# Transposes and grams of two chunks in one break of the TensorE stream, with two-step products on VectorE

## The chip, the cores and the metric

The kernel runs on one core of one Trainium2 chip. The metric is the device time of one execution in microseconds, from the core's first to its last instruction and what lies around it. Matmuls run on TensorE, elementwise work and reductions on VectorE, activations and copies out of PSUM on ScalarE. SyncE issues all DMAs. GpSimd only makes the identity matrix at the start.

## The reference

For each of 2048 rows there are 40 fields of 64 values. All 780 pairs of fields are multiplied elementwise, a small layer with ReLU gives each pair a score, a softmax over the pairs weighs the products, and the weighted sum goes through a last linear layer:

```python
p = x[:, ROW, :]            # ROW, COL: the 780 pairs i < j of 40 fields
q = x[:, COL, :]
inner = p * q
h = relu(einsum('bpe,he->bph', inner, W1) + b1)
logits = einsum('bph,oh->bpo', h, W2) + b2
attn = softmax(logits, axis=1)
pooled = sum(inner * attn, axis=1)
return pooled @ Wl.T + bl
```

All of it is float32.

## The kernel before

Two batch rows, one of each half of the batch, make a *duo*: its 2 x 64 embedding values fill the 128 partitions. A *step* is two duos, a *chunk* eight steps, a *round* 32 steps. There are 512 steps, 64 chunks and 16 rounds.

The work of a chunk: SyncE loads its rows (`load_chunk`, L193). TensorE transposes them with five 128x128 products (`turn_chunk`, L264) into a PSUM slot, and ScalarE copies them to `xt` (`copy_turned`, L353). VectorE appends the first 20 fields of each duo once more (`extend`, L409), so that each pair is a field and a field a fixed shift further, and makes a copy scaled by the last layer's weights (`scale_rows`, L418). TensorE multiplies that copy with `xt` into a 40x40 gram matrix per batch row (`gram_matrix`, L277, 32 products of 40 columns in a chunk). In the profile a float32 product is two records, in the listings of the order below it is one; a transpose is one in both. ScalarE copies the grams out (`copy_gram`, L361). SyncE stores them to DRAM in twelve DMAs (`store_gram`, L204), and loads a whole round of them again in the layout of the logits (`load_gram`, L216): with the gram in hand, the weighted sum and the last layer become a product of the softmax weights with gram entries.

The work of a step: VectorE makes the 2 x 780 pair products in `inner` (`products`: L431 twice, one for each half of the pairs, 760 elements per instruction; at each odd step L438 adds the last ten of each half for both steps). TensorE runs the first layer on them, half by half (`first_layer`, L296, 16 matmuls of 390 columns in a step), ScalarE adds the bias and applies ReLU (`relu`, L369, one per half), and TensorE adds the scores into the bank of the logits (`score`, L316, 8 matmuls), which holds a row for every step of the round. TensorE's order in step s is: layer of s, scoring of s-1, then, where the table names the step, the transposes of a chunk, then the grams of a chunk. ScalarE's order is the two relus, the copies of the same step, then an exponential where it is due.

At the end of a round VectorE copies the logits and takes maxima (`softmax_of_round`, L448 to L460, at step `KEEP_AT` = 7 of the next round), ScalarE takes the exponentials (L377, steps `EXP_AT`), and VectorE multiplies them with the gram and sums (`sums_of_round`, L468 and L476, steps `SUMS_AT`).

The order is written out by hand, by three tables from step to chunk (`turn_after`, `gram_after`, `spread_after`). The engines run freely against each other and are held by semaphores: `inner` is a ring of `INNER_RING` = 8 steps, `hidden` one of 4 steps, `xt` one of 3 chunks, `x_rows` and `gram_rows` have 2 places each, `x_scaled` one. Three PSUM slots are used in turn by everything that TensorE fills (each half of a layer, each chunk's transposes, each chunk's grams), so that each fill waits for the copy or relu of the fill three places before it:

```python
def wait_for_slot(*what):
    if place[what] >= SLOTS:
        pe.wait_ge(slots_emptied, place[what] - SLOTS + 1)
```

SyncE's queue for chunk n is: wait for the transposes of n, load chunk n+2, wait for the copied grams of n, store them; after the last chunk of a round, wait for all stores of the round and load the gram.

## Time and profile before

| | |
|---|---|
| median of 3 runs | 1144.26 us (1144.24 to 1145.02) |
| profiled execution | 1142.66 us |
| its span, first to last instruction | 1140.8 us |
| mean granted TensorE clock | 0.995 of full speed |
| busy: TensorE, VectorE, ScalarE | 1117.5, 1053.8, 981.2 us |
| instructions | 63299 |
| DMA traffic over the span | 45 GB/s |

Busy time counts the stretches in which at least one instruction of an engine is under way, and TensorE's products overlap: a layer record of 0.49 us has seven others beside it. So TensorE's pace is read from the starts of its groups in the timeline, not from the busy share or from the mean length of a record. A row of the timeline merges records of one kind that follow each other; its second number reaches to the modelled end of the last, which lies behind the start of the next group.

### The profile page before, as it was taken

The page shows a single profiled execution, that of the slowest core. Times are in us where ns is not written, and L with a number is a line of the kernel's source. Part 1 is how long each engine was busy: PE and PEld are TensorE (multiplying, and loading weights), DVE is VectorE, ACT ScalarE, POOL GpSimd, SP SyncE. Part 2 cuts the span into 40 slices and gives each one's busy share as a digit, 9 for nine tenths or more (in the row PEclk, how much of TensorE's full clock was granted, in tenths as well). Part 3 has the DMA queues.
Part 4 walks back from the last instruction along what each step waited for, and adds up shares of the span by engine and source line. Part 5 has one row for each costly group of instructions (what it writes and reads, how often), then busy time and mean ns, then how long its engine had stood idle before and what let it go on. Part 6 is the DMA issues. An engine that isn't in the chain of part 4 may idle for free.

```text
span 1140.8 us, 63299 instructions
## 1 busy us (share of the span) xinstructions
PE 1117.5 (98%) x29001; PEld 550.5 (48%) x29001; DVE 1053.8 (92%) x1691; ACT 981.2 (86%) x1219; POOL 0.7 (0%) x6
## 2 busy tenths in 40 slices
PE   6999999999999999999999999999999999999995
PEld 3445444444444444454544544554444444544442
DVE  7999999998999989999899998999999899998983
ACT  5888888888988888888888888888889888898884
POOL 0000000000000000000000000000000000000000
PEclk9999999999999999999999999999999999999998
DMA  2231211312212221122212113122131221222110
GB/s 58 39 70 26 67 30 35 67 29 63 41 29 63 41 56 35 29 65 39 58 35 68 29 34 70 28 64 41 25 67 36 58 39 29 63 41 57 23 25 23
DMA packets 220376, 51.31 MB, mean 45 GB/s; under 512 B 216016, under 2 KB 216016, under 8 KB 220112
## 3 DMA queue, kind: packets, MB, share of 16 engines
q1 hardware_dynamic: 220112, 47.27, 20.2%
q8 instruction: 229, 3.75, 1.4%
q14 instruction: 35, 0.29, 0.1%
HBM read 34.11 MB, written 13.12 MB: 41 GB/s over the span
## 4 chain that ended last, share of the span: by engine, by line
PE 98%; DVE 1%; SPq 1%; DMA 0%; ACT 0%; issue 0%; ACTq 0%
PE slot L296 60%; PE logit_bank L316 30%; PE slot L277 4%; PE slot L264 4%; DMA x_rows<-in_r_x 0%; PE slot L342 0%; SPq L193 0%; ACT hidden L369 0%; DVE weighted L468 0%; SPq L223 0%; SPq L227 0%; SPq L225 0%; SPq L230 0%; DVE logits L448 0%; DVE row_max L452 0%
## 5 line engine op out<-in xcount | busy, mean ns | idle before, releaser
L369 ACT ACTIVATE hidden<-slot,b_col 128x780 f32<-128x780 f32 x1024 | 874.7, 909 | 118.5 <-PE slot L296 118.5
L431 DVE TENSOR_TENSOR inner<-xt 128x760 f32<-128x760 f32 x1024 | 907.8, 943 | 51.3 <-PE slot L296 50.8
L296 PE MATMUL slot<-inner,w_block 64*32 64x390 f32 x16384 | 781.4, 489 | 0.0
L296 PEld LDWEIGHTS slot<-inner,w_block 64*32 64x32 f32 x16384 | 314.1, 107 | 331.0 <-issue 271.3
L316 PE MATMUL logit_bank<-hidden,w_window 64*32 64x390 f32 x8192 | 442.9, 487 | 0.6 <-ACT hidden L369 0.6
L316 PEld LDWEIGHTS logit_bank<-hidden,w_window 64*32 64x32 f32 x8192 | 155.3, 105 | 183.5 <-ACT hidden L369 85.6
L353 ACT COPY xt<-slot 128x640 f32<-128x640 f32 x64 | 44.3, 692 | 20.4 <-PE slot L264 20.4
L264 PE MATMUL slot<-ident,x_rows 128*128 128x128 f32 x320 | 50.1, 288 | 9.7 <-DMA x_rows<-in_r_x 9.7
L438 DVE TENSOR_TENSOR inner<-xt 128x80 f32<-128x80 f32 x256 | 59.4, 232 | 0.0
L264 PEld LDWEIGHTS slot<-ident,x_rows 128*128 128x128 f32 x320 | 34.6, 143 | 49.5 <-issue 44.1
L277 PE MATMUL slot<-xt,x_scaled 64*40 64x40 f32 x4096 | 52.9, 205 | 0.0
L277 PEld LDWEIGHTS slot<-xt,x_scaled 64*40 64x40 f32 x4096 | 45.4, 117 | 11.7 <-issue 11.7
L361 ACT COPY gram_rows<-slot 128x640 f32<-128x640 f32 x64 | 44.4, 693 | 5.9 <-PE slot L277 0.4
L418 DVE TENSOR_SCALAR x_scaled<-xt,wl_col 128x640 f32<-128x640 f32 x64 | 34.8, 544 | 0.0
L448 DVE COPY logits<-logit_bank 128x780 f32<-128x780 f32 x16 | 15.5, 970 | 20.5 <-PE logit_bank L316 20.5
L468 DVE CUSTOM_DVE_ANT_1 weighted<-weight,gram 128x380 f32<-128x380 f32 x32 | 28.0, 874 | 0.8 <-ACT weight L377 0.8
L409 DVE COPY xt<-xt 128x320 f32<-128x320 f32 x64 | 20.3, 317 | 5.8 <-ACT xt L353 5.8
L377 ACT ACTIVATE weight<-logits,exp_bias 128x390 f32<-128x390 f32 x32 | 19.9, 622 | 3.6 <-DVE exp_bias L460 3.6
L452 DVE TENSOR_REDUCE row_max<-logits 128x2 f32<-128x780 f32 x16 | 15.5, 966 | 0.5
L476 DVE CUSTOM_DVE_ANT_0 weighted<-weight,gram 64x10 f32<-64x10 f32 x64 | 10.8, 169 | 1.0
L342 PE MATMUL slot<-ident,stats 128*16 128x128 f32 x8 | 1.9, 416 | 6.0 <-DVE stats L483 6.0
L377 ACT ACTIVATION_READ_ACCUMULATOR weight<-logits,exp_bias 128x1 f32 x32 | 6.4, 201 | 0.0
(28 smaller groups left out, 27.0 us busy)
## 6 DMA issues: line engine op xcount, KB each, us to landing
x_rows<-in_r_x SPq DMA_DIRECT2D x128, 160.0 KB, 3.1
gram<-gram_dram SPq DMA_DIRECT2D x32, 400.0 KB, 3.8
gram_dram<-gram_rows SPq DMA_DIRECT2D x512, 12.5 KB
gram_dram<-gram_rows SPq DMA_DIRECT2D x256, 25.0 KB
w_rows<-in_L_rec_W SPq DMA_DIRECT2D x2, 16.0 KB, 2.3
wl_col<-in_L_rec_Wl SPq DMA_DIRECT2D x2, 0.2 KB, 2.3
b_col<-in_L_rec_b SPq DMA_DIRECT2D x2, 0.2 KB, 2.3
w_window<-in_L_rec_W SPq DMA_DIRECT2D x2, 0.2 KB, 2.3
```

What stands on the lines that cost most here:

```text
L264: last = nc.tensor.transpose(banks_of("turn", n)[:, t * P:(t + 1) * P], x_rows[n % 2][:, t, :, :].rearrange("p h e -> p (h e)"), ident[:, :])
L277: last = nc.tensor.matmul(banks_of("gram", n)[j * TILE:j * TILE + FIELDS, at:at + FIELDS], x_scaled[rows, duo * FIELDS:(duo + 1) * FIELDS] ...
L296: last = nc.tensor.matmul(banks[to:to + QUAD, ab * BANK:ab * BANK + HALF], w1_block[rows, of:of + QUAD], inner[rows, at:at + HALF], start= ...
L316: last = nc.tensor.matmul(logit_bank[g * QUAD:(g + 1) * QUAD, j * BANK:j * BANK + HALF], w2_window[rows, first:first + QUAD], hidden[s % R ...
L353: nc.scalar.copy(window_view(xt[n % XT_RING], 0, [[EXT, CHUNK_DUOS], [TT, U], [1, TT]]), window_view(banks_of("turn", n), 0, [[U, CHUNK_DU ...
L361: nc.scalar.copy(gram_rows[n % 2][:, :, :, :].rearrange("p a m n -> p a (m n)"), banks_of("gram", n)[:, :].rearrange("p (a n) -> p a n", a ...
L369: nc.scalar.activation(hidden[s % RING][:, half * PAIRS:(half + 1) * PAIRS].rearrange("p (a n) -> p a n", a=2), banks_of("layer", s, half) ...
L377: nc.scalar.activation(weight[:, j * HALF:(j + 1) * HALF], logits[:, j * HALF:(j + 1) * HALF], ACT.Exp, bias=exp_bias[:, j:j + 1], accum_o ...
L418: nc.vector.tensor_scalar(x_scaled[:, :].rearrange("p (d f) -> p d f", f=FIELDS), whole[:, :, 0:FIELDS], wl_col[:, 0:1], None, ALU.mult).t ...
L431: nc.vector.tensor_tensor(window_view(inner, to + half * HALF, [[PAIRS, STEP_DUOS], [SPAN, SHIFTS], [1, SPAN]]), window_view(fields, at + ...
L438: nc.vector.tensor_tensor(window_view(inner, to + SHIFTS * SPAN, [[PAIRS, duos], [HALF, 2], [1, LAST]]), window_view(fields, at, [[EXT, du ...
L468: nc.vector.tensor_tensor_reduce(out=weighted[:, 0:main].rearrange("p (d i) -> p d i", i=SPAN), in0=weight[:, of:of + main].rearrange("p ( ...
```

## The change

The chunks are taken in groups of two. The transposes and the grams of a group are issued together, once in sixteen steps: at step 16g - 12 the transposes of chunks 2g and 2g+1 (10 products), and behind them the grams of chunks 2g-2 and 2g-1 (64 products). ScalarE copies them in the same order, two and two. `xt` has four places, `x_scaled` two, `inner` sixteen steps. VectorE makes the products of two steps in one instruction per half, in the order first half, the last ten, second half, so that the layer's first half waits for two instructions and the second for three. The extension and scaling of a chunk are at step 15 of a group and at step 3 of the next, the exponentials at steps 3 and 7 of a round in place of 4 and 5, the sums at 15 and 21 in place of 13 and 14. SyncE loads both chunks of a group, then stores both.

```diff
--- before.py
+++ after.py
@@ -48,8 +48,9 @@
     U = FIELDS // TT
 
     RING = 4
-    INNER_RING = 8
-    XT_RING = 3
+    INNER_RING = 16
+    XT_RING = 4
+    GROUP = 2
     SLOTS = 3
 
     BANK = 512
@@ -82,7 +83,7 @@
         x_rows = [sb(f"x_rows{s}", [P, TT, 2, EMBED]) for s in range(2)]
         xt = [sb(f"xt{s}", [P, CHUNK_DUOS * EXT]) for s in range(XT_RING)]
         inner = sb("inner", [P, INNER_RING * STEP])
-        x_scaled = sb("x_scaled", [P, CHUNK_DUOS * FIELDS])
+        x_scaled = [sb(f"x_scaled{s}", [P, CHUNK_DUOS * FIELDS]) for s in range(GROUP)]
         gram_rows = [sb(f"gram_rows{s}", [P, 2, GRAM_PAIRS, FIELDS]) for s in range(2)]
         gram = sb("gram", [P, STEP_DUOS * SPAN * FIELDS])
         hidden = [sb(f"hidden{s}", [P, STEP]) for s in range(RING)]
@@ -145,18 +146,23 @@
         gram_dram = nc.dram_tensor("gram_dram", (ROUNDS, STEP_DUOS, 2, 2, ROUND_STEPS, SPAN, FIELDS), F32,
                                    kind="Internal").ap()
 
-        def inner_to(s):
-
-            return 5 * (s // 2 + 1)
-
-
-        TURN_AT = -13
-        GRAM_AT = -5
-        SPREAD_AT = -3
-
-        gram_after = {max(n * CHUNK_STEPS + GRAM_AT, 1 + n): n for n in range(CHUNKS)}
-        turn_after = {n * CHUNK_STEPS + TURN_AT: n for n in range(2, CHUNKS)}
-        spread_after = {max(n * CHUNK_STEPS + SPREAD_AT, 1 + n): n for n in range(1, CHUNKS)}
+        def inner_to(s, half):
+
+            return 3 * (s // 2) + 2 + half
+
+
+
+        GROUP_STEPS = GROUP * CHUNK_STEPS
+        TURN_AT = -12
+        GRAM_AT = TURN_AT + GROUP_STEPS
+        SPREAD_AT = [-1, 3]
+
+        def chunks_of(group):
+            return range(group * GROUP, (group + 1) * GROUP)
+
+        gram_after = {g * GROUP_STEPS + GRAM_AT: g for g in range(CHUNKS // GROUP)}
+        turn_after = {g * GROUP_STEPS + TURN_AT: g for g in range(1, CHUNKS // GROUP)}
+        spread_after = {n // GROUP * GROUP_STEPS + SPREAD_AT[n % GROUP]: n for n in range(1, CHUNKS)}
 
 
         place = {("turn", 0): 0, ("weights", 0): 1, ("turn", 1): 2}
@@ -164,9 +170,11 @@
             place["layer", s, 0] = len(place)
             place["layer", s, 1] = len(place)
             if s in turn_after:
-                place["turn", turn_after[s]] = len(place)
+                for n in chunks_of(turn_after[s]):
+                    place["turn", n] = len(place)
             if s in gram_after:
-                place["gram", gram_after[s]] = len(place)
+                for n in chunks_of(gram_after[s]):
+                    place["gram", n] = len(place)
 
         def count_to(*what):
 
@@ -177,8 +185,8 @@
 
 
         KEEP_AT = 7
-        EXP_AT = [4, 5]
-        SUMS_AT = [13, 14]
+        EXP_AT = [3, 7]
+        SUMS_AT = [15, 21]
 
         x_chunks = x.rearrange("(h c b) f e -> h c (b f e)", h=2, b=CHUNK_DUOS).rearrange(
             "h c (p t e) -> h c p t e", p=P, t=TT)
@@ -232,13 +240,15 @@
             for column, value in ((b2_col, b2), (bl_col, bl)):
                 sp.dma_start(column[:, :], value.rearrange("(h o) -> h o", o=1).to_broadcast([P, 1])).then_inc(
                     offsets_loaded, 16)
-            for n in range(CHUNKS):
-                if n + 2 < CHUNKS:
-                    sp.wait_ge(slots_filled, count_to("turn", n))
-                    load_chunk(n + 2)
-                store_gram(n)
-                if n % CHUNKS_PER_ROUND == CHUNKS_PER_ROUND - 1:
-                    load_gram(n // CHUNKS_PER_ROUND)
+            for group in range(CHUNKS // GROUP):
+                for n in chunks_of(group):
+                    if n + 2 < CHUNKS:
+                        sp.wait_ge(slots_filled, count_to("turn", n))
+                        load_chunk(n + 2)
+                for n in chunks_of(group):
+                    store_gram(n)
+                    if n % CHUNKS_PER_ROUND == CHUNKS_PER_ROUND - 1:
+                        load_gram(n // CHUNKS_PER_ROUND)
 
             sp.wait_ge(y_ready, 1)
             sp.dma_start(y_dram, y_out[:, :].rearrange("r (a k) -> r a k", a=2)).then_inc(y_stored, 16)
@@ -276,14 +286,13 @@
                             at = ab * BANK + m * FIELDS
                             last = nc.tensor.matmul(
                                 banks_of("gram", n)[j * TILE:j * TILE + FIELDS, at:at + FIELDS],
-                                x_scaled[rows, duo * FIELDS:(duo + 1) * FIELDS],
+                                x_scaled[n % GROUP][rows, duo * FIELDS:(duo + 1) * FIELDS],
                                 xt[n % XT_RING][rows, duo * EXT:duo * EXT + FIELDS], start=True, stop=True,
                                 tile_position=(ab * TILE, j * TILE))
                 last.then_inc(slots_filled, 1)
 
             def first_layer(s, half):
-                if half == 0:
-                    pe.wait_ge(inner_ready, inner_to(s))
+                pe.wait_ge(inner_ready, inner_to(s, half))
                 wait_for_slot("layer", s, half)
                 banks = banks_of("layer", s, half)
                 for j in range(STEP_DUOS):
@@ -331,9 +340,11 @@
                 if s:
                     score(s - 1)
                 if s in turn_after:
-                    turn_chunk(turn_after[s])
+                    for n in chunks_of(turn_after[s]):
+                        turn_chunk(n)
                 if s in gram_after:
-                    gram_matrix(gram_after[s])
+                    for n in chunks_of(gram_after[s]):
+                        gram_matrix(n)
             score(STEPS - 1)
 
             pe.wait_ge(stats_kept, ROUNDS)
@@ -348,7 +359,7 @@
                 act.wait_ge(slots_filled, count_to("turn", n))
                 if n >= XT_RING:
 
-                    act.wait_ge(inner_ready, inner_to((n - XT_RING + 1) * CHUNK_STEPS - 1))
+                    act.wait_ge(inner_ready, inner_to((n - XT_RING + 1) * CHUNK_STEPS - 1, 1))
                     act.wait_ge(slots_filled, count_to("gram", n - XT_RING))
                 nc.scalar.copy(window_view(xt[n % XT_RING], 0, [[EXT, CHUNK_DUOS], [TT, U], [1, TT]]),
                                window_view(banks_of("turn", n), 0, [[U, CHUNK_DUOS], [1, U], [P, TT]])).then_inc(
@@ -387,9 +398,11 @@
                 relu(s, 0)
                 relu(s, 1)
                 if s in turn_after:
-                    copy_turned(turn_after[s])
+                    for n in chunks_of(turn_after[s]):
+                        copy_turned(n)
                 if s in gram_after:
-                    copy_gram(gram_after[s])
+                    for n in chunks_of(gram_after[s]):
+                        copy_gram(n)
                 for j in range(STEP_DUOS):
                     r, after = (s - EXP_AT[j]) // ROUND_STEPS, (s - EXP_AT[j]) % ROUND_STEPS
                     if r > 0 and after == 0:
@@ -411,35 +424,35 @@
             def scale_rows(n):
                 if n == 0:
                     dve.wait_ge(wl_loaded, 2 * 16)
-                else:
-
-                    dve.wait_ge(slots_filled, count_to("gram", n - 1))
+                if n >= GROUP:
+
+                    dve.wait_ge(slots_filled, count_to("gram", n - GROUP))
                 whole = xt[n % XT_RING][:, :].rearrange("p (d f) -> p d f", f=EXT)
-                nc.vector.tensor_scalar(x_scaled[:, :].rearrange("p (d f) -> p d f", f=FIELDS), whole[:, :, 0:FIELDS],
+                nc.vector.tensor_scalar(x_scaled[n % GROUP][:, :].rearrange("p (d f) -> p d f", f=FIELDS), whole[:, :, 0:FIELDS],
                                         wl_col[:, 0:1], None, ALU.mult).then_inc(scaled_ready, 1)
 
             def products(s):
+
                 n, in_chunk = s // CHUNK_STEPS, s % CHUNK_STEPS
                 if in_chunk == 0:
                     dve.wait_ge(xt_ready, n + 1)
                 if s >= INNER_RING:
-                    dve.wait_ge(slots_filled, count_to("layer", s - INNER_RING, 1))
-                fields = xt[n % XT_RING]
+                    dve.wait_ge(slots_filled, count_to("layer", s + 1 - INNER_RING, 1))
+                fields, duos = xt[n % XT_RING], 2 * STEP_DUOS
                 to = (s % INNER_RING) * STEP
                 at = in_chunk * STEP_DUOS * EXT
                 for half in range(2):
                     nc.vector.tensor_tensor(
-                        window_view(inner, to + half * HALF, [[PAIRS, STEP_DUOS], [SPAN, SHIFTS], [1, SPAN]]),
-                        window_view(fields, at + half * SPAN, [[EXT, STEP_DUOS], [0, SHIFTS], [1, SPAN]]),
-                        window_view(fields, at + half * SPAN + 1, [[EXT, STEP_DUOS], [1, SHIFTS], [1, SPAN]]),
+                        window_view(inner, to + half * HALF, [[PAIRS, duos], [SPAN, SHIFTS], [1, SPAN]]),
+                        window_view(fields, at + half * SPAN, [[EXT, duos], [0, SHIFTS], [1, SPAN]]),
+                        window_view(fields, at + half * SPAN + 1, [[EXT, duos], [1, SHIFTS], [1, SPAN]]),
                         ALU.mult).then_inc(inner_ready, 1)
-                if s % 2:
-                    to, at, duos = to - STEP, at - STEP_DUOS * EXT, 2 * STEP_DUOS
-                    nc.vector.tensor_tensor(
-                        window_view(inner, to + SHIFTS * SPAN, [[PAIRS, duos], [HALF, 2], [1, LAST]]),
-                        window_view(fields, at, [[EXT, duos], [SPAN + LAST, 2], [1, LAST]]),
-                        window_view(fields, at + SPAN, [[EXT, duos], [SPAN + LAST, 2], [1, LAST]]),
-                        ALU.mult).then_inc(inner_ready, 1)
+                    if half == 0:
+                        nc.vector.tensor_tensor(
+                            window_view(inner, to + SHIFTS * SPAN, [[PAIRS, duos], [HALF, 2], [1, LAST]]),
+                            window_view(fields, at, [[EXT, duos], [SPAN + LAST, 2], [1, LAST]]),
+                            window_view(fields, at + SPAN, [[EXT, duos], [SPAN + LAST, 2], [1, LAST]]),
+                            ALU.mult).then_inc(inner_ready, 1)
 
             def softmax_of_round(r):
                 dve.wait_ge(steps_scored, (r + 1) * ROUND_STEPS)
@@ -489,7 +502,8 @@
             dve.memset(w2_window[:, :], 0.0).then_inc(zeroed, 1)
             extend(0)
             for s in range(STEPS):
-                products(s)
+                if s % 2 == 0:
+                    products(s)
                 if s == 1:
                     scale_rows(0)
                 if s in spread_after:
```

TensorE's order around the break at step 11 before. The rows are line, operation, output and input tile, shape and count; `slot` under L264 takes transposes, under L277 grams, under L296 the layer:

```order
L316 MATMUL logit_bank<-hidden,w_window 32x390 x8
L296 MATMUL slot<-inner,w_block 32x390 x16
L316 MATMUL logit_bank<-hidden,w_window 32x390 x8
L264 MATMUL slot<-ident,x_rows 128x128 x5
L277 MATMUL slot<-xt,x_scaled 40x40 x32
L296 MATMUL slot<-inner,w_block 32x390 x16
L316 MATMUL logit_bank<-hidden,w_window 32x390 x8
```

and now, around the break at step 20:

```order
L325 MATMUL logit_bank<-hidden,w_window 32x390 x8
L305 MATMUL slot<-inner,w_block 32x390 x16
L325 MATMUL logit_bank<-hidden,w_window 32x390 x8
L274 MATMUL slot<-ident,x_rows 128x128 x10
L287 MATMUL slot<-xt,x_scaled 40x40 x64
L305 MATMUL slot<-inner,w_block 32x390 x16
L325 MATMUL logit_bank<-hidden,w_window 32x390 x8
```

The transposes and grams stand together twice as long, half as often.

ScalarE's order around the break at step 35 (step 3 of round 1) before:

```order
L369 ACTIVATE hidden<-slot,b_col 128x780 x16
L353 COPY xt<-slot 128x16x40
L361 COPY gram_rows<-slot 128x640
L369 ACTIVATE hidden<-slot,b_col 128x780 x2
L377 ACTIVATE weight,round_stats<-logits,exp_bias 128x390
L369 ACTIVATE hidden<-slot,b_col 128x780 x2
L377 ACTIVATE weight,round_stats<-logits,exp_bias 128x390
L369 ACTIVATE hidden<-slot,b_col 128x780 x12
```

and now, from step 21 on, around the break at step 36 (step 4 of round 1):

```order
L380 ACTIVATE hidden<-slot,b_col 128x780 x30
L388 ACTIVATE weight,round_stats<-logits,exp_bias 128x390
L380 ACTIVATE hidden<-slot,b_col 128x780 x2
L364 COPY xt<-slot 128x16x40 x2
L372 COPY gram_rows<-slot 128x640 x2
L380 ACTIVATE hidden<-slot,b_col 128x780 x6
L388 ACTIVATE weight,round_stats<-logits,exp_bias 128x390
```

The copies stand two and two, and one exponential stands two relus ahead of them, where both stood behind.

VectorE's order around an extension, before:

```order
L431 TENSOR_TENSOR inner<-xt 128x2x380 x4
L438 TENSOR_TENSOR inner<-xt 128x8x10
L409 COPY xt<-xt 128x16x20
L418 TENSOR_SCALAR x_scaled<-xt,wl_col 128x640
L431 TENSOR_TENSOR inner<-xt 128x2x380 x4
L438 TENSOR_TENSOR inner<-xt 128x8x10
```

and now, around those at step 15 and 19:

```order
L445 TENSOR_TENSOR inner<-xt 128x4x380 x2
L451 TENSOR_TENSOR inner<-xt 128x8x10
L445 TENSOR_TENSOR inner<-xt 128x4x380
L422 COPY xt<-xt 128x16x20
L431 TENSOR_SCALAR x_scaled<-xt,wl_col 128x640
L445 TENSOR_TENSOR inner<-xt 128x4x380
L451 TENSOR_TENSOR inner<-xt 128x8x10
L445 TENSOR_TENSOR inner<-xt 128x4x380 x2
```

Products of two steps are two instructions of 4 duos and one for the last ten, where they were four of 2 duos and one.

## Rows read from the trace of the kernel before

**Rows 1.** The page: busy time by engine; granted TensorE clock in 40 slices, in tenths.
```profile
PE 1117.5 (98%) x29001; PEld 550.5 (48%) x29001; DVE 1053.8 (92%) x1691; ACT 981.2 (86%) x1219; POOL 0.7 (0%) x6
...
PEclk9999999999999999999999999999999999999998
```

**Rows 2.** The page: chain that ended last, by engine and line.
```profile
PE slot L296 60%; PE logit_bank L316 30%; PE slot L277 4%; PE slot L264 4%; DMA x_rows<-in_r_x 0%; PE slot L342 0%; SPq L193 0%; ACT hidden L369 0%; DVE weighted L468 0%; SPq L223 0%; SPq L227 0%; SPq L225 0%; SPq L230 0%; DVE logits L448 0%; DVE row_max L452 0%
```

**Rows 3.** Timeline of TensorE around one break: start us, us, engine, line, what, count.
```profile
525.20 0.87 PE L316 MATMUL logit_bank<-hidden,w_window 64*32 64x390 f32 x16
525.99 0.77 PE L264 MATMUL slot<-ident,x_rows 128*128 128x128 f32 x5
526.69 0.83 PE L277 MATMUL slot<-xt,x_scaled 64*40 64x40 f32 x64
527.45 1.54 PE L296 MATMUL slot<-inner,w_block 64*32 64x390 f32 x32
528.78 0.86 PE L316 MATMUL logit_bank<-hidden,w_window 64*32 64x390 f32 x16
529.44 1.52 PE L296 MATMUL slot<-inner,w_block 64*32 64x390 f32 x32
...
538.62 0.86 PE L316 MATMUL logit_bank<-hidden,w_window 64*32 64x390 f32 x16
```

**Rows 4.** Timeline of TensorE at the start: the first layer.
```profile
12.51 3.68 PE L296 MATMUL slot<-inner,w_block 64*32 64x390 f32 x64
```

**Rows 5.** Timeline of TensorE at the start of a round.
```profile
572.02 1.52 PE L296 MATMUL slot<-inner,w_block 64*32 64x390 f32 x32
573.45 0.89 PE L316 MATMUL logit_bank<-hidden,w_window 64*32 64x390 f32 x16
```

**Rows 6.** Timeline of TensorE, cut at 508.90 and 509.05 us: the transposes' ends.
```profile
508.59 0.55 PE L264 MATMUL slot<-ident,x_rows 128*128 128x128 f32 x3
...
508.59 0.66 PE L264 MATMUL slot<-ident,x_rows 128*128 128x128 f32 x4
```

**Rows 7.** The page: groups: busy us, mean ns; the gram's products.
```profile
L277 PE MATMUL slot<-xt,x_scaled 64*40 64x40 f32 x4096 | 52.9, 205 | 0.0
```

**Rows 8.** Timeline of ScalarE around the same break.
```profile
524.91 1.71 ACT L369 ACTIVATE hidden<-slot,b_col 128x780 f32<-128x780 f32 x2 [0.25 <-PE slot L296]
526.79 0.69 ACT L353 COPY xt<-slot 128x640 f32<-128x640 f32 x1 [0.17 <-PE slot L264]
527.58 0.70 ACT L361 COPY gram_rows<-slot 128x640 f32<-128x640 f32 x1
528.50 1.71 ACT L369 ACTIVATE hidden<-slot,b_col 128x780 f32<-128x780 f32 x2 [0.23 <-PE slot L296]
```

**Rows 9.** Timeline of ScalarE: the first exponential of a round and what follows.
```profile
512.74 0.62 ACT L377 ACTIVATE weight<-logits,exp_bias 128x390 f32<-128x390 f32 x1
...
513.34 1.71 ACT L369 ACTIVATE hidden<-slot,b_col 128x780 f32<-128x780 f32 x2
```

**Rows 10.** VectorE: group of the products (page), then timeline around the same break.
```profile
L431 DVE TENSOR_TENSOR inner<-xt 128x760 f32<-128x760 f32 x1024 | 907.8, 943 | 51.3 <-PE slot L296 50.8
...
526.13 0.23 DVE L438 TENSOR_TENSOR inner<-xt 128x80 f32<-128x80 f32 x1
526.28 3.52 DVE L431 TENSOR_TENSOR inner<-xt 128x760 f32<-128x760 f32 x4
```

**Rows 11.** Timeline of VectorE: the copy of the logits at a round.
```profile
572.33 0.97 DVE L448 COPY logits<-logit_bank 128x780 f32<-128x780 f32 x1 [0.30 <-PE logit_bank L316]
```

**Rows 12.** Timeline of the DMA queue of SyncE: stores of one chunk.
```profile
510.89 6.39 SPq L204 DMA_DIRECT2D gram_dram<-gram_rows  x12
```

**Rows 13.** Loads of x (issue ns, then landing us), and SyncE's waits: total, times, longest.
```profile
L193 SPq DMA_DIRECT2D x_rows<-in_r_x x128: 545/625/1757, 0.7 to 1055.8; - x128
...
DMA to landing us min/median/max: 2.5/3.1/5.9
...
SPq L214 <- DMA gram_dram<-gram_rows: 20.0, 15, 3.1
```

## Prediction

> **What bounds the kernel now.** I read the page first: TensorE is busy for 1117.5 us of 1140.8, VectorE for 1053.8 and ScalarE for 981.2, and the granted clock stands at full speed, 2.4 GHz, in all but the last slice [rows 1]. The chain that ended last names TensorE for 98% of the span: the first layer 60%, the scoring 30%, grams and transposes 4% each [rows 2]. So what TensorE has to issue is the time, and the others count where TensorE waits for them. The timeline of TensorE around one chunk's break shows what there is to win [rows 3]. An ordinary step is 32 records of the layer and 16 of the scoring: from 528.78 to 538.62 five of them take 9.84 us, 1.968 each, 0.66 of it from scoring to layer and so 1.31 from layer to scoring. Where transposes and a gram stand in between, scoring to scoring is 528.78 - 525.20 = 3.58 us, so a break costs 3.58 - 1.97 = 1.61 us. Its pieces, start to start: scoring to first transpose 0.79 us, where scoring to layer is 0.66 (0.135 extra); five transposes 0.70; the gram 0.76; and the layer behind it takes 1.33 in place of 1.31 (0.02). Check on the whole: the first layer starts at 12.51 us [rows 4]; 512 steps x 1.968, 62 breaks x 1.615, two breaks with a gram alone (0.92 each) and 15 waits of 0.12 us at the rounds (the layer takes 573.45 - 572.02 = 1.43 us there) [rows 5] add 1111 us, and that leaves 17 us of the span for the first step's own waits and for the end behind the last scoring. TensorE has next to no other wait in its steady state.
>
> **The change part by part.** *Breaks.* The 62 breaks with 5 transposes and 64 gram records (32 products) become 31 with 10 and 128; the two gram-only breaks (steps 1 and 499) become one with two grams, at step 500. What does a second chunk cost when it stands right behind the first? Cutting the timeline inside the transposes, three of them end at 0.55 us and four at 0.66 [rows 6], so one more costs 0.11 us and five more 0.55. The gram's 64 records are 0.83 us from first start to last end and 0.205 us each [rows 3, 7], so the last starts 0.625 us in and 64 more cost 0.63. A double break is 0.135 + (0.70 + 0.55) + (0.76 + 0.63) + 0.02 = 2.795 us, against 2 x 1.615 = 3.23: 0.435 saved, 31 times, is **13.5 us**. The gram-only ones: 2 x 0.915 before, 0.915 + 0.63 now, **0.3 us** saved. What goes is the change of form: about 0.14 us from scoring to transposes, 0.15 from transposes to gram (0.70 - 0.55), 0.13 from gram to layer (0.76 - 0.63). The bounds of the double break are 3.23 us (the second chunk costs as much as the first, nothing won) and the 2.795; I take the low end, since second halves, steps and steps behind steps of one form run without a seam in the rows although each has waits of its own.
> The Trainium skill (TensorEngine Tiling (Array Packing), Key Properties) says that changing the tiling mode drains TensorE. The row shows less than a drain: the transposes start at 525.99, before the scoring's modelled end at 526.07 [rows 3]. Were each switch a whole drain, a switch would be worth the distance from the next free start to the modelled end, 526.07 - 525.86, 526.76 - 526.59 and 527.52 - 527.32, some 0.21, 0.17 and 0.20 us, and the sum would be the rival below.
> *ScalarE.* It now copies four tiles in a row, two turned chunks and two grams. Let t be the start of the transposes. The step's relus end at t+0.63, the first copy starts at t+0.80 as now [rows 8], the others follow at 0.69 us each: done at t+1.49, 2.18, 2.88 (the first gram is ready at t+2.14) and 3.57. With three slots, each place waits for the one three before it. The second gram (t+1.88) waits for the first copy: 0.39 us to spare. The layer's first half (t+2.64) waits for the second copy: 0.46. Its second half (t+3.30) waits for the third: 0.42. The relu of the first half is ready at t+3.69 (1.05 us behind the layer, as 528.50 - 527.45), and ScalarE is free at t+3.57. So nothing is left of the backlog: cost 0. *Exponentials.* They move from steps 4 and 5, behind the break at step 3, to steps 3 and 7, around the break at step 4. One takes 0.60 us of ScalarE (512.74 to 513.34), where 0.25 was idle per step [rows 8, 9]; the relus of the break's step end some 0.25 us later, a little behind t+0.88, and the copies some 0.1 later, which the 0.39 covers. Cost 0, at the worst 0.1 x 15.
> *VectorE.* Two instructions of 760 elements become one of 1520. An instruction's pitch is (3.52 - 0.94)/3 = 0.86 us for 760 elements (0.94 us is what one lasts), and 0.15 for the 80 behind them [rows 10], so an element costs 1.04 ns and an instruction 0.067 us besides. Two fewer in two steps save 0.134 us, in a round of 32 steps 2.1 us. VectorE waited for TensorE's layer 50.8 us in all [rows 10], 3.2 in each of 16 rounds. A round is to get 2 x 0.435 = 0.9 us shorter, so VectorE keeps 3.2 + 2.1 - 0.9 = 4.4 us to spare, and its saving is off the path: 0 for the end. It now idles elsewhere: with sixteen places its lead over TensorE is bounded by the maxima at step 7 (the last scoring of the round before must be done), about 7 steps or 13.8 us ahead. Behind that come a copy of 0.97 us, three instructions no longer than it (at most 3.9 in all) and 3.5 of products before step 8 is needed, so no layer waits. The other waits leave it further ahead: the extension of the chunk at step 15 needs a copy of step 4, the sums at 15 and 21 need exponentials of steps 3 and 7. The products' first half now releases a layer's first half, and a place is released a step later; with a lead of 7 to 14 steps both are worth 0. The 0.12 us at each round's first scoring stays: the copy of the logits (0.97 us, 0.30 us behind the scoring) is longer than the layer beside it covers [rows 5, 11].
> *SyncE.* The stores of two chunks now follow one another, 24 issues, and stand in front of the next loads of x. From t+3: 2 x 6.4 us of issue at the longest, at a round's end up to 3.1 us until the stores have landed, then six loads (two of the gram, four of x) at 0.63 each, 3.8, and at most 5.9 to landing [rows 12, 13]: t+28.6 at the latest. The next transposes are 16 steps and a break later, t+34.2. Covered by over 5 us. At step 500 no transposes stand ahead, so the stores begin at t+2 and the gram's last loads have landed by t+25, worked out alike; the last scoring ends eleven steps later, at t+24 or after, and the copy, the maxima and the exponentials (over 2 us) stand between it and the sums. *Start and end.* The first layer stands behind the same transposes of chunk 1 and waits for fewer products than before; behind the last scoring nothing is changed. Both 0.
> **Sum:** -13.5 - 0.3 = -13.8 us on the profiled execution's 1142.66, so 1128.9. The median of the runs is 1144.26, 1.6 above it; at its level **1130.5 us**.
>
> **Rivals.** *The copies hold TensorE (slower).* If the layer behind a double break waited for the last of the four copies, not for the second, it would start at t+3.6 and not at t+2.64: +0.96 per break against -0.435, 31 x 0.52 = +16 us, 1160. It decides once the wait exceeds 0.435 us per break, that is when ScalarE is 0.9 us later than I worked out. Against it: the margins of 0.39 to 0.46 and no backlog at the end [rows 8]. 3%. *Nothing is won.* The second chunk costs as much as the first, since each has its own wait for a slot and, for the transposes, for x: 1144, no change. Against it: the seamless halves of the layer. 3%. *A whole drain per switch.* Each pair saves 0.21 + 0.17 + 0.20 + 0.02 = 0.60, 31 times is 18.6, and 0.3 beside it: 1144.3 - 18.9 = 1125.4. Against it: transposes that start before the modelled end [rows 3]. 4%. *Loads of x come late* behind 24 stores. The price is what exceeds those 5 us, in each of 15 rounds: 15 x 2 us would be 1160. 1%. *The clock falls in the longer break.* TensorE has stood at 2.4 GHz through 62 breaks of 1.6 us with narrow products [rows 1]; the new ones are 2.8 us. If the clock fell to 1.2 GHz behind each, one step at half speed costs 1.97 us, 31 times 61 us: 1191. It decides from 0.22 of a step per break. 1%, since no slice of the steady state shows a fall. [...] *Another wait on VectorE or a slot* that I did not see, some 2 to 5 us of the 13.8, is within my forecast.
>
> **How the numbers follow.** The forecast, with the waits just named, has 88% and its own range is 1127 to 1135: below, 0.5 us per gram-and-transpose term read too high and the spread of runs (0.8 us); above, the exponentials' 1.5 us and some 3 us of waits. The rest takes 12%: 4 + 3 + 3 + 1 + 1. The range that holds 8 in 10 is that of the forecast, 1127 to 1135. A change of 0.2%, 2.3 us, is about what a measurement of this kernel can tell from none. Faster: forecast 88 and whole drain 4, 92%. Same: 3%. Slower: 5%.
>
> **What would show it.** TensorE's timeline: a break of 10 and 128 records, scoring to scoring 4.76 us (1.97 + 2.79) instead of 3.58, transposes to gram 1.25, gram to layer 1.39; ordinary steps stay at 1.97. VectorE: products of 1.73 us in half the number, total busy down by some 30 us, and waits of several us for scoring at the maxima in place of those for the layer. ScalarE: four copies in a row. Wrong if TensorE's rows show waits for a copy, for x or for products, if the layer behind the break takes over 1.4 us, or if the granted clock dips.

## Result and the profile after

The changed kernel took 1159.70 us (median of 6 runs, 1158.03 to 1165.16), the kernel before 1144.25 us (6 runs on the same chip, 1143.54 to 1145.02): a ratio of 1.0142, 95% interval 1.012 to 1.0164. It is slower by 15 to 16 us, where the forecast was 14 us faster. The profiled execution took 1159.47 us (span 1157.7), against the 1128.9 that the sum gave for it.

The page of the changed kernel; its lines answer to [rows 1, 2, 10]:

```profile
PE 1119.6 (97%) x29001; PEld 637.2 (55%) x29001; DVE 1010.8 (87%) x1179; ACT 978.9 (85%) x1219; POOL 0.7 (0%) x6
...
q8 instruction: 231, 3.78, 1.4%
...
PE 96%; DVE 2%; issue 1%; SPq 1%; DMA 0%; ACT 0%; ACTq 0%
...
L305 PE MATMUL slot<-inner,w_block 64*32 64x390 f32 x16384 | 867.2, 489 | 9.0 <-issue 8.8
L445 DVE TENSOR_TENSOR inner<-xt 128x1520 f32<-128x1520 f32 x512 | 874.4, 1734 | 0.6
...
L461 DVE COPY logits<-logit_bank 128x780 f32<-128x780 f32 x16 | 15.5, 971 | 131.1 <-PE logit_bank L325 131.1
```

VectorE changed as forecast in kind: 512 instructions of 1734 ns, total busy down by 43 us (forecast: some 30), and its waiting now stands at the copy of the logits at the maxima (131.1 us in 16 times, that is at L461, where 50.8 us stood at the products before [rows 10]). The granted clock stands at nine tenths or more in every slice but the last. The new thing is on TensorE: an "issue" in its idle time, 8.8 us at the layer and 5.5 us at the gram, which the kernel before doesn't have. The waits of TensorE by what it waited for say the same; the kernel before has no line with "issue" there:

```profile
PE slot L274 <- DMA x_rows<-in_r_x: 9.6, 2, 5.1
PE slot L305 <- issue: 8.8, 11, 1.7
...
PE slot L287 <- issue: 5.5, 3, 2.2
```

TensorE's timeline (start us, us, engine, line, what, count) shows two kinds of break. From one scoring to the next, beyond an ordinary step's 1.97 us, 15 of the 31 breaks cost 2.81 to 2.87 us, close to the 2.795 of the prediction, here the one at step 84:

```profile
200.94 0.86 PE L325 MATMUL logit_bank<-hidden,w_window 64*32 64x390 f32 x16
201.73 1.31 PE L274 MATMUL slot<-ident,x_rows 128*128 128x128 f32 x10
202.97 1.48 PE L287 MATMUL slot<-xt,x_scaled 64*40 64x40 f32 x128
204.38 1.54 PE L305 MATMUL slot<-inner,w_block 64*32 64x390 f32 x32
205.72 0.86 PE L325 MATMUL logit_bank<-hidden,w_window 64*32 64x390 f32 x16
```

Scoring to scoring takes 205.72 - 200.94 = 4.78 us, transposes to gram 1.24, gram to layer 1.41. Twelve cost 3.9 to 5.5 us and four 2.95 to 3.34, and these, all but the one at step 436 (3.06), have a pause in or behind them, as the one at step 68:

```profile
162.51 0.89 PE L325 MATMUL logit_bank<-hidden,w_window 64*32 64x390 f32 x16
163.34 1.31 PE L274 MATMUL slot<-ident,x_rows 128*128 128x128 f32 x10
164.58 1.33 PE L287 MATMUL slot<-xt,x_scaled 64*40 64x40 f32 x113
168.12 0.36 PE L287 MATMUL slot<-xt,x_scaled 64*40 64x40 f32 x15 [2.22 <-issue]
168.41 1.86 PE L305 MATMUL slot<-inner,w_block 64*32 64x390 f32 x32
169.98 1.59 PE L325 MATMUL logit_bank<-hidden,w_window 64*32 64x390 f32 x16
171.28 2.33 PE L305 MATMUL slot<-inner,w_block 64*32 64x390 f32 x32
173.40 0.86 PE L325 MATMUL logit_bank<-hidden,w_window 64*32 64x390 f32 x16
```

TensorE stops for 2.22 us *inside* a gram, behind its 113th record, where the program has no wait. In most of these breaks it stops inside the layer behind the grams. **Where** it stops is the clue. Count all records of TensorE in order of time, matmuls, weight loads and waits. From 20 us to the last break, outside a stretch at half clock (below), two records that follow one another lie more than 0.42 us apart at 19 places, and all 19 have the same number modulo 256: the pause stands behind records 256 apart or a multiple of it. These 19 hold 23.0 us, with the ordinary distance of their records. (Below 0.42 us a distance says little: over 2000 records stand 0.2 to 0.42 us behind the one before them, at any number, and most of those cost no time.) In the kernel before, none is over 0.42 us. And 256 instructions are what one packet of the queue of instructions carries: 3.78 MB in 231 packets are 16.4 KB each, and TensorE's records come out at just that number of blocks: 59,174 / 256 = 231 here, 58,662 / 256 = 229 in the kernel before, whose page has 229 packets, and 65,658 / 256 = 256 in e5 below, whose page has 256. The page's line for the kernel before:

```profile
q8 instruction: 229, 3.75, 1.4%
```

So the theory after this reading: TensorE's program comes from memory in blocks of 256 instructions, the next block begins to come only when the last is entered, and two grams in a row (128 matmuls and 128 weight loads in 1.4 us) use up a block before the next has come.

The queues of the DMA engines support it. In three cuts of the same stretch there is a packet of instructions at 158.25 us, then none in 158.3 to 165.3, then one that begins at 165.33 (first line: 158.0 to 158.5; second: 158.3 to 165.3; third: 165.3 to 166.6; packets, MB, share):

```profile
q8 instruction: 1, 0.02, 16.6%
...
DMA packets 0, 0.00 MB, mean 0 GB/s; under 512 B 0, under 2 KB 0, under 8 KB 0
...
q8 instruction: 1, 0.02, 6.0%
```

That packet takes 1.25 us; TensorE, which stopped at 165.70, goes on at 168.12, some 1.5 us after the packet's end. (By the starts the stop is 2.42 us long, by the timeline, which counts from the modelled end of the last matmul, 2.22. I give starts below.) SyncE's stores don't hold up the start of the packet, as they begin behind it:

```profile
166.18 8.88 SPq L212 DMA_DIRECT2D gram_dram<-gram_rows  x18
```

Every block of all twelve traces fits this. Take each record at that number as the first of a block, from the second such record on, and set the packets of the queue of instructions beside them in order, one to each. At these 2802 places TensorE never started the block's first record earlier than 1.19 us after the end of its packet. At the pauses over 0.42 us the distance is 1.2 to 1.6 us, elsewhere it goes up to some 5 us. And the packet of the block after it never began more than 0.21 us ahead of that first record, so TensorE never had more than one block in hand beyond the one it was in. A pause is the stretch in which TensorE is through with one block and the next has just come.

By this theory a pause depends on where the block's end falls. Measured from the first record of the grams to the block's end, in records, the breaks of this execution sort themselves: from -29 to 80 records, pauses of 0.8 to 2.4 us; 84 to 121, up to 0.8, and these in the step behind; 141 to 208, none. Since a group of sixteen steps has some 1848 records, that place moves on by 56 from break to break, and so pauses come and go with a rhythm of four or five breaks.

### The profile page after: what moved, and what is told of

Same layout as the page of the kernel before. It is cut to its first block, busy times and chain, and to the rows that moved or that the text cites. A ratio compares the mean times of both kernels' runs of the same rounds, so it can differ in the third digit from the quotient of the medians.

```text
span 1157.7 us, 63282 instructions
## 1 busy us (share of the span) xinstructions
PE 1119.6 (97%) x29001; PEld 637.2 (55%) x29001; DVE 1010.8 (87%) x1179; ACT 978.9 (85%) x1219; POOL 0.7 (0%) x6
## 3 DMA queue, kind: packets, MB, share of 16 engines
q8 instruction: 231, 3.78, 1.4%
## 4 chain that ended last, share of the span: by engine, by line
PE 96%; DVE 2%; issue 1%; SPq 1%; DMA 0%; ACT 0%; ACTq 0%
PE slot L305 59%; PE logit_bank L325 29%; PE slot L287 4%; PE slot L274 3%; DVE inner L445 1%; DMA x_rows<-in_r_x 0%; DVE logits L461 0%; DVE row_max L465 0%; PE slot L353 0%; SPq L201 0%; ACT hidden L380 0%; DVE weighted L481 0%; SPq L231 0%; SPq L233 0%; SPq L235 0%
## 5 line engine op out<-in xcount | busy, mean ns | idle before, releaser
L305 PE MATMUL slot<-inner,w_block 64*32 64x390 f32 x16384 | 867.2, 489 | 9.0 <-issue 8.8
L445 DVE TENSOR_TENSOR inner<-xt 128x1520 f32<-128x1520 f32 x512 | 874.4, 1734 | 0.6
L305 PEld LDWEIGHTS slot<-inner,w_block 64*32 64x32 f32 x16384 | 389.8, 107 | 322.7 <-issue 222.9
L325 PE MATMUL logit_bank<-hidden,w_window 64*32 64x390 f32 x8192 | 528.5, 488 | 1.0 <-ACT hidden L380 0.6
L325 PEld LDWEIGHTS logit_bank<-hidden,w_window 64*32 64x32 f32 x8192 | 191.6, 105 | 141.8 <-issue 52.1
L461 DVE COPY logits<-logit_bank 128x780 f32<-128x780 f32 x16 | 15.5, 971 | 131.1 <-PE logit_bank L325 131.1
L287 PE MATMUL slot<-xt,x_scaled 64*40 64x40 f32 x4096 | 48.4, 205 | 5.5 <-issue 5.5
L274 PE MATMUL slot<-ident,x_rows 128*128 128x128 f32 x320 | 43.3, 283 | 9.6 <-DMA x_rows<-in_r_x 9.6
L364 ACT COPY xt<-slot 128x640 f32<-128x640 f32 x64 | 41.3, 696 | 12.7 <-PE slot L274 12.6
```

What stands on the lines that cost most here:

```text
L274: last = nc.tensor.transpose(banks_of("turn", n)[:, t * P:(t + 1) * P], x_rows[n % 2][:, t, :, :].rearrange("p h e -> p (h e)"), ident[:, :])
L287: last = nc.tensor.matmul(banks_of("gram", n)[j * TILE:j * TILE + FIELDS, at:at + FIELDS], x_scaled[n % GROUP][rows, duo * FIELDS:(duo + 1 ...
L305: last = nc.tensor.matmul(banks[to:to + QUAD, ab * BANK:ab * BANK + HALF], w1_block[rows, of:of + QUAD], inner[rows, at:at + HALF], start= ...
L325: last = nc.tensor.matmul(logit_bank[g * QUAD:(g + 1) * QUAD, j * BANK:j * BANK + HALF], w2_window[rows, first:first + QUAD], hidden[s % R ...
L364: nc.scalar.copy(window_view(xt[n % XT_RING], 0, [[EXT, CHUNK_DUOS], [TT, U], [1, TT]]), window_view(banks_of("turn", n), 0, [[U, CHUNK_DU ...
L445: nc.vector.tensor_tensor(window_view(inner, to + half * HALF, [[PAIRS, duos], [SPAN, SHIFTS], [1, SPAN]]), window_view(fields, at + half ...
```

## Experiments

Each kernel is compared with the kernel before on the same chip.

| kernel | what differs from the changed kernel | us, median (range) | ratio to before, 95% |
|---|---|---|---|
| e1_group_only | products of one step each | 1158.18 (1156.08 to 1161.42) | 1.0109 to 1.0146 |
| e2_products_only | breaks of one chunk, as before | 1145.01 (1143.42 to 1145.56) | 0.9998 to 1.0017 |
| e3_grams_split | second gram four steps later | 1139.67 (1138.90 to 1141.34) | 0.9953 to 0.9976 |
| e4_apart | both grams four steps after the transposes | 1160.26 (1158.83 to 1161.83) | 1.0128 to 1.0159 |
| e5_filled_in_step | some 200 records of waits more per group | 1222.57 (1217.04 to 1223.70) | 1.0652 to 1.0702 |
| e6_filled_shifted | the same, block's end elsewhere | 1235.38 (1232.41 to 1235.40) | 1.0776 to 1.0808 |
| e7_transposes_between | gram, ten transposes, gram | 1140.34 (1139.29 to 1141.65) | 0.9957 to 0.9982 |
| e8_shifted_once | 120 records of waits more in all | 1159.47 (1157.88 to 1163.90) | 1.0122 to 1.0159 |
| e9_split_step_products | e3 with products of one step | 1138.94 (1137.96 to 1139.73) | 0.9942 to 0.9967 |
| e10_between_step_products | e7 with products of one step | 1139.57 (1137.89 to 1141.16) | 0.9947 to 0.9974 |

### One half of the change at a time

e1, against the changed kernel (the products as before):

```diff
-            return 3 * (s // 2) + 2 + half
+            return 5 * (s // 2 + 1)
...
-                pe.wait_ge(inner_ready, inner_to(s, half))
+                if half == 0:
+                    pe.wait_ge(inner_ready, inner_to(s, half))
...
-                if s % 2 == 0:
-                    products(s)
+                products(s)
```

> Only the grouping is kept (pairs of chunks in one break, new places of extension, exponentials and sums, the rings of sixteen and four); VectorE makes the products step by step again and the layer's second half has no wait of its own. Theory (instruction fetch): the 256 TensorE instructions of two grams in a row are used up in some 1.4 us, faster than the next 256 arrive, so the gaps with nothing released stay, after every second or so break: 1155 to 1165 us. Rival (the products of two steps, their coarser release or the layer's second wait cost the time): 1130 to 1133 us.

e2, against the kernel before:

```diff
-    INNER_RING = 8
+    INNER_RING = 16
...
-            return 5 * (s // 2 + 1)
+            return 3 * (s // 2) + 2 + half
...
-                products(s)
+                if s % 2 == 0:
+                    products(s)
```

> Only the products of two steps, the sixteen inner places and the layer's second wait, with one chunk per break as in the kernel before. Theory (instruction fetch): no break holds more than 128 gram records, no gaps, 1142 to 1146 us. Rival (coarser products or 512 more wait instructions on TensorE cost the time): 1155 to 1175 us.

The whole loss goes with the grouping, 1158.18 us (18 pauses over 0.42 us at that number, 21.1 us); the two-step products alone cost nothing that can be measured. They were worth 43 us of VectorE and no time, as VectorE had 50.8 us to spare [rows 10].

### The two grams apart, the break otherwise the same

e3:

```diff
-        gram_after = {g * GROUP_STEPS + GRAM_AT: g for g in range(CHUNKS // GROUP)}
+        gram_after = {n // GROUP * GROUP_STEPS + GRAM_AT + 4 * (n % GROUP): n for n in range(CHUNKS)}
```

> The changed kernel with its ten transposes together, but the two grams four steps apart. Theory (instruction fetch): never more than 128 gram records in a row, no gaps over 0.5 us; a pair of chunks costs 0.135+1.25+0.76+0.02 and 0.135+0.76+0.02, 3.08 us in place of 3.23, so 1144.3 - 31x0.15 = 1139 to 1141 us, faster than both kernels. Rival (the row of ScalarE copies, the stores of two chunks, or the pair's places): still 1150 to 1160.

e4, the pair of grams still together but four steps away from the transposes:

```diff
-        gram_after = {g * GROUP_STEPS + GRAM_AT: g for g in range(CHUNKS // GROUP)}
+        gram_after = {g * GROUP_STEPS + GRAM_AT + 4: g for g in range(CHUNKS // GROUP)}
```

> The changed kernel with the two grams together but four steps after the ten transposes. Theory (instruction fetch): the two grams in a row are as dense as before, and the sparse transposes no longer stand in the same 256 instructions, so the gaps stay or grow: 1160 to 1175 us. Rival (the length of the break, or four copies in a row on ScalarE): the break is cut in two, no gaps, 1132 to 1137 us.

e3 is 20 us faster than the changed kernel and 4 us faster than before, although it has *more* changes of form per group than the changed kernel. Its two breaks, at steps 84 and 88:

```profile
196.77 0.86 PE L324 MATMUL logit_bank<-hidden,w_window 64*32 64x390 f32 x16
197.56 1.31 PE L273 MATMUL slot<-ident,x_rows 128*128 128x128 f32 x10
198.80 0.83 PE L286 MATMUL slot<-xt,x_scaled 64*40 64x40 f32 x64
199.56 1.54 PE L304 MATMUL slot<-inner,w_block 64*32 64x390 f32 x32
200.89 0.86 PE L324 MATMUL logit_bank<-hidden,w_window 64*32 64x390 f32 x16
...
206.79 0.86 PE L324 MATMUL logit_bank<-hidden,w_window 64*32 64x390 f32 x16
207.59 0.83 PE L286 MATMUL slot<-xt,x_scaled 64*40 64x40 f32 x64
208.34 1.54 PE L304 MATMUL slot<-inner,w_block 64*32 64x390 f32 x32
209.68 0.86 PE L324 MATMUL logit_bank<-hidden,w_window 64*32 64x390 f32 x16
```

They cost 200.89 - 196.77 - 1.97 = 2.15 and 209.68 - 206.79 - 1.97 = 0.92 us, 3.07 together against 2 x 1.615 = 3.23 in the kernel before. In all of e3 one pause over 0.42 us is left. e4 has its four copies broken up into two and two and a shorter break, and lost as much as the changed kernel: 18 pauses over 0.42 us, 15.3 us, now behind a pair of grams that stands alone:

```profile
32.38 1.48 PE L287 MATMUL slot<-xt,x_scaled 64*40 64x40 f32 x128
33.79 1.53 PE L305 MATMUL slot<-inner,w_block 64*32 64x390 f32 x29
36.34 0.52 PE L305 MATMUL slot<-inner,w_block 64*32 64x390 f32 x2 [1.02 <-issue]
```

So neither the transposes nor the length of the break are needed for the loss, and two grams in a row are enough for it.

### Same break, same work, another order inside it

e7, in the placing, on TensorE and on ScalarE alike:

```diff
+        def break_after(s):
+            grams = [("gram", n) for n in chunks_of(gram_after[s])] if s in gram_after else []
+            turns = [("turn", n) for n in chunks_of(turn_after[s])] if s in turn_after else []
+            return grams[:1] + turns + grams[1:]
...
-                if s in turn_after:
-                    for n in chunks_of(turn_after[s]):
-                        turn_chunk(n)
-                if s in gram_after:
-                    for n in chunks_of(gram_after[s]):
-                        gram_matrix(n)
+                for what, n in break_after(s):
+                    (turn_chunk if what == "turn" else gram_matrix)(n)
```

> The changed kernel with the break's order gram, ten transposes, gram. One change of form more than in the changed kernel, 0.14 us: a pair costs 2.93 in place of 3.23 us, 31 x 0.30 = 9 us less than the kernel before. Theory (instruction fetch): 276 instructions of a break take 2.8 us and not 256 in 1.4, so at most short gaps where the boundary falls badly (some 0.3 us in a third of the breaks): 1135 to 1141 us. Rival (the length of the break or the four copies in a row): 1155 or more.

```profile
161.52 0.89 PE L326 MATMUL logit_bank<-hidden,w_window 64*32 64x390 f32 x16
162.34 0.83 PE L288 MATMUL slot<-xt,x_scaled 64*40 64x40 f32 x64
163.10 1.31 PE L275 MATMUL slot<-ident,x_rows 128*128 128x128 f32 x10
164.34 0.83 PE L288 MATMUL slot<-xt,x_scaled 64*40 64x40 f32 x64
165.10 1.54 PE L306 MATMUL slot<-inner,w_block 64*32 64x390 f32 x32
166.44 0.86 PE L326 MATMUL logit_bank<-hidden,w_window 64*32 64x390 f32 x16
```

This is the cleanest pair of the study. e7 issues the same instructions in the same break, with one change of form more (166.44 - 161.52 - 1.97 = 2.95 us against 2.81), the same four copies in a row on ScalarE and the same 24 stores, and it is 19 us faster. The ten transposes put 1.24 us with few instructions between two stretches with many; 4 pauses over 0.42 us that hold 3.3 us are left of 19 and 23.0. It rules out the copies, the stores and the length of the break as causes.

### Moving the block's end

e5 and e6 add waits that are long met to TensorE's stream (two waits in a row make one instruction and one record; the counts here are of records), so that a group has a whole number of blocks and their end always falls in the same place: in the middle of the grams, 158 to 173 records in, where the changed kernel had no pause (e5), or at 38 to 53, where it had pauses of 0.8 to 1.4 us (e6). They add work and leave nothing out.

```diff
+            met = [(w1_loaded, 32), (xt_ready, 1), (zeroed, 1), (b1_loaded, 32), (wl_loaded, 32), (w2_loaded, 32),
+                   (ident_ready, 1), (offsets_loaded, 32), (x_loaded[0], 32), (x_loaded[1], 32)]
...
+            def pad(count):
+                for semaphore, value in met[:count]:
+                    pe.wait_ge(semaphore, value)
...
+                count = 8 if s > 4 else 0
+                more = 485 <= s < 500
```

In e6 the last line reads `more = 5 <= s < 20`, which moves 120 of the records from the end to the start.

> The changed kernel with some 200 more TensorE instructions per pair of chunks, all of them waits that are long met, spread twelve to a step, so that two breaks lie a multiple of 256 instructions apart and the 256-instruction boundary falls into the middle of every gram pair (158 to 173 instructions after its first). The work, the order, ScalarE's four copies in a row and the 24 stores are unchanged. Theory (instruction fetch): in the changed kernel no break with the boundary at 141 to 208 had a gap, so none has one here: 1129 to 1135 us, the time that was predicted, if the added instructions cost nothing. Rival (any cause in the order of work, the copies or the stores): no better than the changed kernel, 1158 or more, since only instructions were added.

> The same kernel with the same number of instructions, but 120 of the met waits stand in the second group of steps and not in the last, so that the boundary falls 38 to 53 instructions after the first gram instruction in every break from the second on, and the next one shortly behind the pair. Theory (instruction fetch): the 256 instructions between the two boundaries hold over 200 of the grams', and each break has a gap of 1.1 to 1.5 us, as those of the changed kernel with the boundary there: 31 x 1.3 = 40 us above the kernel before this one in the job, 1168 to 1180. Rival (the position in the instruction stream does not matter): the same time as that kernel within 2 us.

Both **missed** by far. The order was right (e6 is 13 us slower than e5), the sizes were not. Over a group there are now 128 records per step instead of 115.5. Pauses stand at the block's end in e5 too (38 over 0.42 us, 39.0 us in all; e6 44, 41.4 us), in the gram where none was expected, and the packets begin later: in e5 half of those before a pause begin more than 2.7 us behind the start of the block before. A step with twelve records more took 1.97 us as before (median). Those with some sixteen more, two in each group, took 0.2 and 0.4 us longer (medians), and the fifteen with twenty more 0.5 to 1.1 us. So the added waits cost time beside the pauses; why the packets begin later isn't shown.

As a test of position they are inconclusive; the tool disturbed what it was to measure. e8 is the gentle form: 120 records of waits in ten early steps and none after, which shifts every later block's end by 120 records at no lasting cost, and names beforehand which breaks pause.

```diff
+                count = 8 if 6 <= s < 16 else 0
```

> The changed kernel with some 120 met waits in steps 6 to 15 alone, between the first and the second break, so that every later break stands 120 instructions further on in TensorE's stream than in the changed kernel; nothing else. Counting breaks from 0 (break k is at step 16k+4). Theory (instruction fetch, boundaries every 256 instructions): gaps of 0.7 us or more where the boundary lies from 30 before to 80 behind the first gram instruction, which is now at breaks 1, 2, 5, 6, 10, 11, 14, 15, 19, 20, 23, 24, 28 and 29, and none at 0, 3, 7, 8, 12, 16, 17, 21, 25, 26 and 30; in the changed kernel 3, 7, 8, 12, 16, 17, 21, 25, 26 and 30 had gaps. The total is that of the changed kernel, 1157 to 1163 us. Rival (a gap belongs to a place in the program, such as what the other engines or the DMAs do at that break): the same breaks as in the changed kernel.

Breaks are counted from 0, at step 4. Of the 14 named to pause, 12 did (0.89 to 2.26 us; break 2 had 0.13 and break 11 none, with the block's end at 220 and 224 records); of the breaks 0, 3, 7, 8, 12, 16, 17, 21, 25, 26 and 30, named to run free, none did (0.02 us at most over the records' ordinary distance), while in the changed kernel 3, 7, 8, 12, 16, 17, 21, 25, 26 and 30 had pauses of 0.8 to 1.9 us each. Break 3 in the changed kernel, and the same break in e8:

```profile
128.54 1.48 PE L287 MATMUL slot<-xt,x_scaled 64*40 64x40 f32 x128
129.95 0.87 PE L305 MATMUL slot<-inner,w_block 64*32 64x390 f32 x13
131.67 1.17 PE L305 MATMUL slot<-inner,w_block 64*32 64x390 f32 x18 [0.84 <-issue]
```

```profile
129.28 1.48 PE L287 MATMUL slot<-xt,x_scaled 64*40 64x40 f32 x128
130.69 1.54 PE L305 MATMUL slot<-inner,w_block 64*32 64x390 f32 x32
132.02 0.86 PE L325 MATMUL logit_bank<-hidden,w_window 64*32 64x390 f32 x16
```

Break 6 is the other way round, a pause of 0.53 us in the changed kernel and of 2.26 in e8:

```profile
234.22 1.47 PE L287 MATMUL slot<-xt,x_scaled 64*40 64x40 f32 x125
237.74 0.27 PE L287 MATMUL slot<-xt,x_scaled 64*40 64x40 f32 x3 [2.06 <-issue]
```

The same program text at the same step stops or doesn't, by its number alone. The total stayed the same (1159.47), as a shift only changes which breaks are hit. The copies, the loads of x and the stores at these breaks are the same in both kernels.

### What is left to win

e9 and e10 are e3 and e7 with the products of the kernel before:

> The kernel with transposes in pairs and the grams four steps apart, with VectorE's products step by step as before and without the layer's second wait. Theory (the grouping of the transposes is the whole gain, VectorE has time to spare): 1137.5 to 1140 us, the same as with products of two steps or 1 us less, as the first steps start sooner. Rival (the products of two steps are part of the gain): 1141 to 1145.

> The kernel with the break's order gram, ten transposes, gram, with VectorE's products step by step and without the layer's second wait, so 512 TensorE instructions fewer. Theory (instruction fetch): the break still costs 2.92 us, and the short gaps of 0.2 to 0.3 us behind a third of the breaks grow fewer: 1136 to 1139.5 us. Rival (the products of two steps are part of the gain): 1141 to 1145.

e9 is the fastest kernel of the study, 1138.94 us, 5 us under the kernel before. In its trace no pause over 0.42 us is left between 20 us and the last break, and its waits of TensorE have no line with "issue". Its gain comes from the transposes, ten in a row. Its 31 breaks with transposes and a gram cost 67.4 us over ordinary steps and its 33 grams by themselves 0.92 each, 97.7 in all; in the kernel before 62 breaks cost 100.7 and the two single grams 1.9. That is 4.8 us less, against 5.2 by the medians. What grouping the grams as well was to save, no run had without pauses. That e9 and e10 beat e3 and e7 by 0.7 and 0.8 us is less than the runs of each kernel differ among themselves, and says nothing firm of the layer's second wait or of the two-step products.

## Why the prediction was wrong

*Breaks, the term of 13.5 us.* The working of a double break from the seams was right to 0.02 us at best and 0.08 at worst where nothing else came in: 2.81 to 2.87 us measured, 2.795 forecast. Its bounds were wrong: the 31 double breaks cost 107.2 us, 3.46 each, above the 3.23 that stood as the upper bound. **The failed step is the reason given for the low end**, "second halves, steps and steps behind steps of one form run without a seam". It took what holds for steps of few, long instructions to hold for two grams in a row. A step has 96 matmuls and weight loads in 1.97 us, 256 in over 5 us; two grams have 256 in 1.4 us. The rows of before held the warning in [rows 7], 4096 matmuls of the gram with as many weight loads in short breaks, and in the page's line of the queue of instructions (above), which I didn't read. What I left out is a cost by the number of instructions: in the kernel before, the fastest 256 records take 3.1 us and never pause; in the changed kernel the fastest take 1.3 us. Had "instructions per us" been a row of the sum beside "us of work", the upper bound would have been open.

The account of the miss, on the profiled execution, 1159.47 - 1128.9 = 30.6 us, by the distance of one step's scoring from the next: 107.2 - 31 x 2.795 = 20.6 us are in the breaks themselves; 0.8 at step 500, where two grams stand alone; 2.8 in ordinary steps shortly behind a break, where pauses of the same kind fell; 1.5 in the step at half clock (below). 2.5 us stand at the rounds, where seven of the first scorings cost 0.3 to 0.6 us in place of 0.12, and 1.4 in seven steps of 0.2 each (40, 104 and so on); these 3.9 us I haven't traced; e9 has none of them. The rest is under 1 us.

*ScalarE, 0.* Right. The rows after a break without a pause answer to [rows 8]: four copies without idle time between them, and the layer's relu waits for TensorE by 0.23 us as before, so there was no backlog.

```profile
202.53 1.29 ACT L364 COPY xt<-slot 128x640 f32<-128x640 f32 x2 [0.17 <-PE slot L274]
203.86 1.34 ACT L372 COPY gram_rows<-slot 128x640 f32<-128x640 f32 x2
205.44 1.71 ACT L380 ACTIVATE hidden<-slot,b_col 128x780 f32<-128x780 f32 x2 [0.23 <-PE slot L305]
```

*VectorE, 0.* Right, by e2 and by its waits on the page. Its own saving was sized too low, some 34 us (2.1 a round) against 43 measured, which cost the forecast nothing. *SyncE, 0.* Right: TensorE's waits for x are the two at the start, as before. *Start and end, 0.* Right within half a us: the first scoring starts at 16.76 us, in the kernel before at 16.01 with 0.94 us lost in the step behind it, and from the last scoring to the end both take 15.7.

*The rivals.* The right number, 1160, stood with the copies (3%) and with the loads of x (1%), and neither happened: e7 has the same copies and stores and is fast. A price that comes out right is no evidence for its mechanism. A whole drain per switch would have given a double break of 3.23 - 0.60 = 2.63 us; the shortest took 2.81. The clock fell in one break only. The rivals were made of what the program names, slots, transfers and waits, and of the clock; the one that came is in none of its lines.

The Trainium skill (Runtime: NRT & Kernel Launch, Instruction fetch mechanics) describes this fetch: blocks of 16 KiB, 256 instructions, the next taken in while the current one runs. The trace agrees on the size of the blocks. The page also says that crossing a block costs "one DMA tail-bump, mostly hidden", and there the measurement decides otherwise: hidden in the kernel before at 3.1 us a block and more, but over 20 us of 1160 in the changed one.

**What stays open.** No run changed the fetch itself; it is inferred from the number modulo 256, from the packets, and from e8. Of the 19 pauses of the changed kernel, 15 have a packet that begins 0.4 to 1.2 us behind the start of the block before, one at that start, and three 1.9 to 2.5 us behind it (these are among the four longest pauses). Why it comes late there, I can't say. Density isn't all of it either: the one pause of e3 (0.86 us) stands behind a block that had lasted 5.0 us, with a packet that began 2.7 us into it. Nor did e5 settle what rate of instructions the fetch can sustain.

## What to carry to other kernels

Where many small products stand in a row, count instructions as well as microseconds: matmul and weight load are one each, and a stretch that uses 256 of them faster than a block has been seen to come (no pause in the kernel before, whose fastest took 3.1 us; pauses with 1.4) can stop TensorE for 1 to 2 us at a place where the program has no wait. A pause with "issue" as its reason whose record numbers agree modulo 256 points to this. The remedy here costs little: put work of few, long instructions between the dense stretches (e7), or leave them steps apart (e3, e9), and batch only what is sparse in instructions, such as the transposes.

## What the runs showed of the hardware

- In the changed kernel TensorE stops 0.5 to 2.4 us at 19 ends of a block of 256 instructions. Behind a pause it goes on 2.3 to 3.8 us after the start of the block before, in three cases 4.4 to 5.2 us, with a packet of 0.9 to 1.3 us in between. From the packet's end to the first record it is 1.2 to 1.6 us, and in none of the twelve traces less than 1.19.
- Waits that are long met aren't free on TensorE when there are many. e5 is 63 us slower than the changed kernel, of which 16 stand in more and longer pauses at the block's end; twelve records of them in an ordinary step cost nothing, twenty 0.5 to 1.1 us.
- Behind the pause at step 68, 2.42 us, inside the grams, the granted clock fell to half, 1.2 GHz, for 3.4 us, and one step took 3.42 us instead of 1.97. The view by windows shows it (busy us of the five engines, then the granted clock, the DMA share and GB/s). Pauses up to 1.98 us in the same trace left it alone. The length of the pause isn't the whole of it: in e8 it fell behind one of 2.02 us (0.67 from 1047 to 1052 us) and not behind the one of 2.26, in e1 behind one of 2.17 us and not behind the one of 2.37.

```profile
160.00:169.40 9.40, 7.18 (x250) 4.58 (x241) 9.40 (x8) 6.56 (x11) 0.00 (x0) 1.00 0.09 13
169.40:172.80 3.40, 3.40 (x56) 1.44 (x48) 3.40 (x6) 1.79 (x2) 0.00 (x0) 0.51 0.22 32
172.80:176.00 3.20, 3.20 (x86) 1.40 (x76) 3.13 (x9) 2.63 (x4) 0.00 (x0) 0.98 0.30 44
```
